# First two edge stages each sum the attributes of half of a group's columns, on the kernel with folded biases

## The reference, cut to what matters

```python
# layer 0 (two GCN layers): sums of messages over the edges into each node
msg = x[src] * ew[:, None]; agg = segment_sum(msg, dst, n)            # twice
# layer 1: messages x[dst] summed by src
# layer 2: sums of the edges' own attributes, the same at whatever point they are made
aggregated = segment_sum(edge_attr_128, dst, num_segments=n)
h = concat([x, aggregated]) @ W1 + b1; out = silu(layer_norm(h)) @ W2 + b2
# layer 3 (two layers): reflected messages, summed by dst
h_ref = x[src] - 2 * dot(x[src], rel[type]) * rel[type]
```

## Time and profile before

| | us |
|---|---|
| median of three runs | 4166.23 (4159.86 to 4170.01) |
| the profiled execution | 4162.3 (span 4160.5) |
| PE busy | 3536.3 (85% of the span) |
| DVE busy | 3183.2 (77%) |
| POOL busy | 2943.0 (71%) |
| ACT busy | 2582.3 (62%) |
| `l0a`, first to last product | 395.2 to 791.8 |
| `l0b`, first to last product | 1092.6 to 1356.9 |
| mean granted clock of TensorE | 0.953 of full |

### The profile page before, as it was taken

The page is one execution under the profiler, slowest core; times in us unless marked ns, Lnnn a source line. Parts: engine busy times, 40 slices in busy tenths (PEclk is TensorE's granted clock), DMA queues, the critical chain, the costliest instruction groups (busy, mean ns, idle before and its releaser), DMA issues.

```text
span 4160.5 us, 79758 instructions
## 1 busy us (share of the span) xinstructions
PE 3536.3 (85%) x18468; PEld 2206.8 (53%) x18576; DVE 3183.2 (77%) x11794; ACT 2582.3 (62%) x5498; POOL 2943.0 (71%) x3125
## 2 busy tenths in 40 slices
PE   5674999999678999687899999996688775789997
PEld 2211444588433566333799999996234442234454
DVE  7654755466865788854688888887997999987998
ACT  5593257633136788644587778786156774267888
POOL 3765554477776899777566666664775998775888
PEclk8795999999899999899999999998899998999999
DMA  3334467788346788555555555552477885577887
GB/s 82 84 97 76 136 203 233 263 281 281 120 132 233 253 285 288 167 155 178 173 182 180 180 179 180 182 183 84 121 217 237 263 263 166 151 233 261 289 288 233
DMA packets 532695, 810.51 MB, mean 195 GB/s; under 512 B 126084, under 2 KB 180550, under 8 KB 532254
## 3 DMA queue, kind: packets, MB, share of 16 engines
q1 hardware_dynamic: 392991, 545.93, 42.3%
q10 hardware_dynamic: 85166, 154.99, 10.0%
q0 software_dynamic: 54096, 104.47, 9.5%
HBM read 493.19 MB, written 311.11 MB: 193 GB/s over the span
## 4 chain that ended last, share of the span: by engine, by line
PE 51%; DVE 19%; POOL 14%; issue 8%; DMA 3%; DVEq 2%; ACT 2%; POOLq 1%; ACTq 0%; SPq 0%
PE ps L1661 14%; DVE hit L1122 4%; PE ps L1825 4%; POOL records_by_dst L695 4%; POOL got L746 4%; PE ps L1806 4%; PE ps L1807 4%; POOL rstd L781 3%; PE ps L1728 2%; PE ps L1727 2%; PE ps L1785 2%; PE ps L1786 2%; PE ps L1816 2%; PE ps L1694 2%; PE ps L1743 2%
## 5 line engine op out<-in xcount | busy, mean ns | idle before, releaser
L1661 PE MATMUL ps<-hit,rest 128*128 128x512 bf16 x2296 | 714.5, 392 | 94.7 <-DVE hit L1122 89.5
L781 POOL TENSOR_TENSOR rstd<-vare,neg_half 128x4 f32<-128x4 f32 x490 | 557.6, 1138 | 218.0 <-DVE vare L1187 182.1
L1661 PE MATMUL ps<-hit,got 128*128 128x512 bf16 x1148 | 451.1, 393 | 221.2 <-DVE hit L1122 84.4
L1388 ACT ACTIVATE evac<-ps 128x512 f32<-128x512 f32 x392 | 234.2, 597 | 642.8 <-PE ps L1661 634.0
L746 POOL DMA_INDIRECT got<-nodes_l,sorted_by_dst x392 | 400.0, 1020 | 132.6 <-issue 112.5
L1661 PEld LDWEIGHTS ps<-hit,got 128*128 x1172 | 117.0, 100 | 562.2 <-issue 466.1
L1215 DVE TENSOR_TENSOR nT<-sums,ps 128x512 f32<-128x512 f32 x392 | 263.0, 671 | 171.1 <-PE ps L1706 137.1
L1373 ACT ACTIVATE ps<-zeros 128x512 f32<-128x512 f32 x588 | 344.3, 598 | 59.3 <-DVEq L443 34.1
L1661 PEld LDWEIGHTS ps<-hit,rest 128*128 x2344 | 234.9, 100 | 241.3 <-issue 36.1
L746 POOL DMA_INDIRECT got_pair<-in_x,sorted_by_dst x196 | 197.3, 1007 | 201.9 <-PE ps L1661 130.8
L1410 ACT ACTIVATE aff<-ps,shift,rstd 128x128 f32<-128x128 f32 x784 | 290.8, 447 | 1.3 <-POOL shift L797 1.2
(11 more groups left out here) (298 smaller groups left out, 10101.0 us busy)
## 6 DMA issues: line engine op xcount, KB each, us to landing
nodes_l<-xout SPq DMA_DIRECT2D x196, 256.0 KB, 3.2
xin<-nodes_l SPq DMA_DIRECT2D x196, 256.0 KB, 3.7
sums<-sums_l SPq DMA_DIRECT2D x196, 256.0 KB, 2.9
sums_l0a<-evac_pair ACTq DMA_DIRECT2D x98, 256.0 KB
sums_l<-evac_pair ACTq DMA_DIRECT2D x98, 256.0 KB
sums<-sums_l0a SPq DMA_DIRECT2D x98, 256.0 KB
sums_l0b<-evac ACTq DMA_DIRECT2D x98, 256.0 KB
sums<-sums_l0b SPq DMA_DIRECT2D x98, 256.0 KB
```

The source lines that it names most:

```text
L781: pool.tensor_tensor(rstd[:, n, at, :], vare[:, n, at, :], neg_half[:, :], ALU.pow)\
L1388: act.activation(w.evac[h][:, slot, :], ps[:, BANKS * h + g % BANKS, :], ACT.Copy).then_inc(s["out"].sem, 1)
L1661: last = pe.matmul(into, part.rearrange("p a d -> p (a d)"), w.hit[:, w.place(i), :], start=False, stop=False, skip_group_check=True)
```

## The change: what it does

`l0a` and `l0b` are both paired. In each step of `l0a` the attributes' three matmuls use columns 0 to 255 of the hit matrix, in `l0b` columns 256 to 511, so an attribute matmul is 256 columns wide. ACT zeroes, copies and stores only these columns of the attribute banks, in both stages. The `tail` buffers go: the third part of both halves lies in `rest`, as in the single stages. Both paired stages have 100 hits, a ring of 16 tiles and 3 output slots. SP loads every attribute batch in both stages, and in `l0b` issues the reload behind these loads. Since bank 6 is now used in `l0b`, PE waits there until ACT has copied out the last group before it turns the keys (`groups_out`). The number of `free` increments is corrected to those that POOL makes.

```diff
-HITS_PAIR = 96
+HITS_PAIR = 100
+ATTR_COLUMNS = {"l0a": (0, 256), "l0b": (256, 512)}
...
-                self.tail = [] if not pair else [held(f"tail{name}{n}", [P, ring, 2 * D], BF16) for n in range(1 + pair)]
-                self.evac = [held(f"evac{name}{n}", [P, evacs, ROWS]) for n in range(1 + pair)]
+                self.evac = [held(f"evac{name}{n}", [P, evacs, (ROWS, ROWS // 2)[n]]) for n in range(1 + pair)]
...
-        paired = Window("_pair", early, RING_PAIR, HITS_PAIR, EVAC_PAIR, True)
+        paired = {n: Window(f"_{n}", at, RING_PAIR, HITS_PAIR, EVAC_PAIR, True) for n, at in (("l0a", early), ("l0b", base))}
...
-        BUFFERS = {name: paired if name == "l0a" else single for name in WINDOWS}
+        BUFFERS = {name: paired.get(name, single) for name in WINDOWS}
...
-                    for h, _ in halves:
-                        last = act.activation(ps[:, BANKS * h + g % BANKS, :], zeros[:, :], ACT.Copy)
+                    for h, _, lo, hi in halves:
+                        last = act.activation(ps[:, BANKS * h + g % BANKS, 0:hi - lo], zeros[:, 0:hi - lo], ACT.Copy)
...
-                        into = ps[:, BANKS * h:BANKS * h + BANKS, :][:, bass.ds(bank, 1), :].rearrange("p a n -> p (a n)")
+                        lo, hi = ATTR_COLUMNS[name] if h else (0, ROWS)
+                        into = ps[:, BANKS * h:BANKS * h + BANKS, :][:, bass.ds(bank, 1), 0:hi - lo].rearrange("p a n -> p (a n)")
                         for part in (w.got_hi[h][:, bass.ds(slot, 1), 1:2 * D:2], w.rest_hi[h][:, bass.ds(slot, 1), 1:2 * D:2],
-                                     w.third[h][:, bass.ds(slot, 1), 0:D * w.step:w.step]):
-                            last = pe.matmul(into, part.rearrange("p a d -> p (a d)"), w.hit[:, w.place(i), :], start=False, stop=False,
+                                     w.rest_hi[h][:, bass.ds(slot, 1), 0:2 * D:2]):
+                            last = pe.matmul(into, part.rearrange("p a d -> p (a d)"), w.hit[:, w.place(i), lo:hi], start=False, stop=False,
...
                 if name == "l0b":
+                    groups_out(pe, "d1", GROUPS)
                     keys_of_tiles("src")
```

More of the change, by code:

```diff
@@ L268, in __init__ @@
                 self.rest = [held(f"rest{name}{n}", [P, ring, D]) for n in range(1 + pair)]
-                self.tail = [] if not pair else [held(f"tail{name}{n}", [P, ring, 2 * D], BF16) for n in range(1 + pair)]
-                self.evac = [held(f"evac{name}{n}", [P, evacs, ROWS]) for n in range(1 + pair)]
+                self.evac = [held(f"evac{name}{n}", [P, evacs, (ROWS, ROWS // 2)[n]]) for n in range(1 + pair)]
                 self.got_hi = [buf[:, :, :].bitcast(BF16) for buf in self.got]
                 self.rest_hi = [buf[:, :, :].bitcast(BF16) for buf in self.rest]
[L273 to L276, removed]
+                self.low = [buf[:, :, 0:2 * D:2] for buf in self.rest_hi]
+                self.hit_at, self.end = at, held.at
             def free_below(self, end):
@@ L389, in edge_totals @@
             rel_loads = 16 * (WINDOWS[name][3] == "rel")
-            made = {"hit": STEPS, "msg": BATCHES, "zero": GROUPS, "step": STEPS, "out": GROUPS * (1 + w.pair), "free": BATCHES * w.pair,
+            made = {"hit": STEPS, "msg": BATCHES, "zero": GROUPS, "step": STEPS, "out": GROUPS * (1 + w.pair), "free": (BATCHES - w.ring // K) * w.pair,
                     "refl": BATCHES * (rel_loads > 0)}
@@ L585, in edges @@
                         at = b * K % RING_PAIR
-                        sp.dma_start(paired.got[1][:, at:at + K, :].bitcast(I32), attr[:, b * K:b * K + K, FIELDS:FIELDS + D])\
+                        sp.dma_start(BUFFERS[name].got[1][:, at:at + K, :].bitcast(I32), attr[:, b * K:b * K + K, FIELDS:FIELDS + D])\
                           .then_inc(s[f"side{b % 4}"].sem, 16)
@@ L1367, in edges @@
                 w = BUFFERS[name]
-                halves = ((0, sum_d[name]), (1, sum_d["l2"]))[0:1 + w.pair]
+                lo, hi = ATTR_COLUMNS.get(name, (0, 0))
+                halves = ((0, sum_d[name], 0, ROWS), (1, sum_d["l2"], lo, hi))[0:1 + w.pair]
                 def clear(g):
-                    for h, _ in halves:
-                        last = act.activation(ps[:, BANKS * h + g % BANKS, :], zeros[:, :], ACT.Copy)
+                    for h, _, lo, hi in halves:
+                        last = act.activation(ps[:, BANKS * h + g % BANKS, 0:hi - lo], zeros[:, 0:hi - lo], ACT.Copy)
                     last.then_inc(s["zero"].sem, 1)
@@ L1386, in edges @@
                     act.wait_ge(s["step"].sem, done[g % 4] & 511)
-                    for h, _ in halves:
-                        act.activation(w.evac[h][:, slot, :], ps[:, BANKS * h + g % BANKS, :], ACT.Copy).then_inc(s["out"].sem, 1)
+                    for h, _, lo, hi in halves:
+                        act.activation(w.evac[h][:, slot, :], ps[:, BANKS * h + g % BANKS, 0:hi - lo], ACT.Copy).then_inc(s["out"].sem, 1)
                     act.wait_ge(*s["out"](len(halves) * (g + 1)))
@@ L1391, in edges @@
                         clear(g)
-                    for h, dest in halves:
-                        act.dma_start(dest[g * P:(g + 1) * P, :], w.evac[h][:, slot, :]).then_inc(s[f"st{slot}"].sem, 16)
+                    for h, dest, lo, hi in halves:
+                        act.dma_start(dest[g * P:(g + 1) * P, lo:hi], w.evac[h][:, slot, :]).then_inc(s[f"st{slot}"].sem, 16)
             def norm(phase, dest, done, free, rows=None, n=0, ready="rstd", behind=0):
```

## The result

The changed kernel takes 4234.4 us (median of four runs, 4231.3 to 4236.3), the kernel before 4165.8 us on the same occasions. The ratio is 1.0167, 95% interval 1.0153 to 1.0181: slower by 1.7%, clear of noise. The forecast was 4234 us. The profiled execution of the changed kernel has a span of 4234.2 us, 73.7 more than before; the medians differ by 68.6.

The account below looks back on a forecast made before the run. PE bounds the kernel, its array in `l0a` and its sequencer in late `l0b`; afterwards the sequencer paces both. -37 + 96 + 4 + 4 + 1 = +68 us on 4162.3 gives 4230, as a median 4234 us; range 4204 to 4268.

Parts of the forecast that it names:

- The bound: PE limits both stages before the change: its array in `l0a` (5.22 us a quad), its sequencer in late `l0b` (3.21).
- The quad of 4.67 us: Sequencer's time per quad (four steps) in both paired stages: 3.21 us plus 12 register operations, 1.46 us; bounds 4.45 to 4.9.
- small terms: In each paired stage, 2 us for POOL's gathers and the early ring, 2 us for ACT stalls at the end.
- 256 columns at 0.11 us: PE's array takes 0.11 us per bf16 matmul of 256 columns; bounds 0.108 and 0.216 us.
- The start: DVE sets the pace of both stages until the sixth batch is ready: 44.4 us instead of 42.7.
- The new wait: PE waits for ACT's last two copies before turning the keys after `l0b`: +1 us.
- The reload: Sorted records reloaded behind `l0b`'s last attribute load: 16.7 us, issued about 35 us before the end, hidden by 18 us.
- Array sets the pace: Rival: the array bounds both paired stages at 3.91 us a quad, about -31 us, 4135 us; chance 0.06.
- break-even of 4.17 us a quad: Quad time at which both paired stages together gain nothing; no change to be told at 4.1 to 4.25 us, chance 0.04.
- Short ring: Rival: 16 tiles too short for the gathers, PE stalls in both stages' first 20 batches, +40, 4274 us; chance 0.10.
- Half the width saves nothing: Rival: 256-column matmuls take as long as 512, array quad 5.18 us, +70, 4304 us; chance 0.03.

Follow-up runs that it names:

- the hoisted one: Changed kernel, paired stages' operand addresses computed ahead of a step's six matmuls, 3 register operations a step instead of 7: 4151.2 us.
- the longer ring: Changed kernel with addresses computed ahead of the matmuls in all stages, plus 32-tile rings and 79 hits in both paired stages: 4116.4 us.

## Why the prediction was right

**The bound.** That `l0a` was bound by the array and late `l0b` by the sequencer was read from the distance of the quads' marks against 12 or 24 times 0.216 us. For the paired stages of the changed kernel, the one with 64 columns and the hoisted one confirm it from both sides: taking work from the array did not shorten the time, taking operations from the sequencer did. For late `l0b` of the kernel before it is half right. With its addresses hoisted that kernel keeps 3.18 us a quad there, because POOL's gathers set the pace of that stage. The prediction passed over POOL, since it is busy for only 75 of 117 us; but the issue gaps between its gathers are not in that figure, and 5.0 us a batch stood in the earlier trace rows. It took the 3.21 us as the sequencer's price alone. That this could be carried over to the paired stage was luck: the sequencer's own price, 3.1 us a quad early in `l1`, happens to lie close to it.

**The quad of 4.67 us.** Measured: 4.73 and 4.77. The sum of parts (late `l0b`'s 3.21 and 12 operations at 0.122) was 0.06 to 0.10 us short, 4 to 7 us a stage. The small terms for the early ring and for stalls late in a stage, 4 us a stage, made up for this in the sum. That they are the same time is not shown.

**256 columns at 0.11 us.** This was taken from the f32 product of `d0`, and the bf16 matmuls of 256 columns measured 0.11 us too. For 256 columns the Trainium skill, TensorE: Matmul & The Clock Gate, section Back-to-back issue gap, has 262 cycles, 109 ns, and the trace agrees with its 0.11 us. As the kernels with 64 and 384 columns show, the width did not matter for the time.

**The start.** 44.4 us were forecast from DVE's first operation on the first batch to the sixth batch ready, 1.7 more than before. The rows that begin and end this time in `l0a`:

```profile
389.23 0.67 DVE L1135 TENSOR_TENSOR got_l0a<-got_l0a,sorted_by_dst 128x512 f32<-128x512 f32 x1
...
433.13 1.11 DVE L1120 TENSOR_SCALAR hit_l0a<-node_of,node_at_dst 128x512 bf16<-128x512 f16 x4
```

They are 43.9 us apart, 42.7 before: the start has grown by 1.2 us, not 1.7.

**The new wait.** Forecast +1:

```profile
1422.41 0.38 PE L1661 MATMUL ps<-hit_l0b,rest_l0b 128*128 128x256 bf16 x2
1423.76 0.33 PE L1594 MATMUL ps<-ident,keys_s 128*128 128x128 f32 x1 [0.96 <-ACT evac_l0b L1387]
```

The idle 0.96 us for ACT's copies was not there before. The turn now starts 1.2 us behind the start of the last product instead of 0.2.

**The reload.** Forecast: about 35 us before the end, hidden. SP's transfer and DVE's first use of it, tile `sorted_by_src` in `l0b`:

```profile
L522 SPq DMA_DIRECT2D sorted_by_src<-records_by_src x1: 557/557/557, 1384.6 to 1384.6; - x1
L1030 DVE COPY keys_s<-sorted_by_src x1: 334/334/334, 1401.3 to 1401.3; 128x196 f32<-128x196 f32 x1
...
DMA to landing us min/median/max: 5.3/5.3/5.3
```

It was issued 38 us before the last product and took 5.3 us, where the prediction took 16.7 from the earlier trace rows: priced too high. The cover was larger than reckoned.

**The rivals.** *Array sets the pace* fell with the quads' marks and the 64 columns; with the sequencer relieved in all stages the kernel took 4135.7 us, within a microsecond of the 4135 that this rival had been given. That is a coincidence: the single stages gave some 15 us of it and the paired ones less. The 4135 is also added up wrongly. With the prediction's own terms -45 + 5 + 5 + 4 + 4 + 1 is -26, and the time 4140. The break-even of 4.17 us a quad does hold up: with the hoisted paired stages at 4.11 us the kernel is 12 us faster than the kernel before. *Short ring:* it costs 9 us in `l0b` of the kernel before, and 19 us in both stages when the sequencer is out of the way (with the hits and the attribute loads changed too). That it is hidden behind the sequencer in the changed kernel is argued from the quad's 4.73 to 4.77 us; no run gave that kernel a longer ring. The 40 us that I had for it were twice too much. *Half the width saves nothing* fell with the 0.11 us.

**What was right partly by luck.** The forecast hit the median within 1 us, but the profiled executions, for which the sum was made, differ by 74 and not 68 us. Some 7 us of the 74 are in stages that did not change, and without them the sum is 67. That the 3.21 us of late `l0b` could stand for the sequencer alone was luck, as said above. What the rest of pairing costs `l0b` (306 us without any attribute matmul, where the prediction has DVE and the new loads hidden) I did not foresee. It did not count, because the sequencer's quads took longer still. Had they not, `l0b` would have ended later than the first rival's sum said: the hoisted kernel's `l0b` takes 322 us, that sum has 1401 - 1093 = 308 and 5 for POOL.

## What to carry to other kernels

Moving work from a stage where the array is full to one where it has gaps gains only if the gaps are the array's to fill. Compare the distance between rounds with the array's own sum. If it is larger, look for the sequencer's operations in the view of the source line; an engine's busy time does not count them. Splitting a matmul in two of half the width keeps the columns and doubles the hand-overs, addresses and weight loads; price the sequencer's round as well as the array's. Compute dynamic addresses next to each other, ahead of the matmuls, so that they fuse. And when a pace is taken as the price of one part, ask what else arrives at that pace: in late `l0b` POOL's batches did.

## What the runs showed of the hardware that I had not expected

Register operations that stand between matmuls follow each other every 0.12 us, the hand-over of the matmuls between them included (28 in 3.3 us). Fusing 28 operations a quad into 12, ahead of the same 24 matmuls, took 0.62 us off a quad (4.73 to 4.11), and 0.75 us with the longer ring (3.98). That is 0.04 to 0.05 us for each of the 16 that went, and a lower bound, since the array takes over near 3.9 us. How the 0.12 us divide between the operation and the hand-over is not shown. One table load of eight numbers takes 0.59 us of the sequencer.

The granted clock of the hoisted kernel was 0.98 of full between 600 and 700 us. This is not the fuller array: the kernel before had PE busy 99% of `l0a` at 1.00. It is one stretch at the lower of the two levels, 1.2 instead of 2.4 GHz, right behind a wait of 3.5 us for ACT:

```profile
693.38 0.38 PE L1667 MATMUL ps<-hit_l0a,rest_l0a 128*128 128x256 bf16 x2
697.25 0.61 PE L1667 MATMUL ps<-hit_l0a,got_l0a 128*128 128x512 bf16 x1 [3.48 <-ACT ps L1372]
...
699.14 0.63 PE L1667 MATMUL ps<-hit_l0a,got_l0a 128*128 128x512 bf16 x1
699.57 0.97 PE L1667 MATMUL ps<-hit_l0a,rest_l0a 128*128 128x512 bf16 x2
```

```profile
697.00:700.40 3.40, 3.15 (x10) 1.36 (x11) 1.41 (x6) 1.81 (x5) 0.00 (x0) 0.51 1.06 403
```

The granted clock is 0.51 there, and matmuls of 512 columns start 0.43 us apart (699.14 to 699.57) instead of 0.216.
